# Attention with 128 steps of scores, exponentials and values: issuing probabilities times values for two key tiles together

## The chip, the cores and the metric

The kernel runs on 1 core of one Trainium2 chip. The metric is device microseconds (us) of one execution of the whole program; the time before is a median of three runs.

## The reference

x is 1024 tokens by 512 features. It is layer-normed to xn. An attention branch projects xn to 32 query heads and 8 key/value heads of 16 features each (four query heads share one key/value head), applies rotary embedding to queries and keys, and computes softmax(q k^T / 4) v over all 1024 keys, without a mask. A dense branch computes z = xn W^T + b, a low-rank product m with a clamped ratio of norms as its factor, and silu of the sum. The output is x + attention * silu(dense).

```python
scores = jnp.einsum('bqhd,bkhd->bhqk', q, k) / jnp.sqrt(jnp.float32(D))
probs = jax.nn.softmax(scores.astype(jnp.float32), axis=-1)
out = jnp.einsum('bhqk,bkhd->bqhd', probs, v).reshape(B, S, E)
...
x = x + s * g
```

## The kernel before

**Groups, steps and heads.** After a part that normalises, projects, rotates and splits queries and keys into bf16 parts (to about 104 us), the attention goes through KV = 8 groups g (one key/value head and its four query heads). A group has 16 steps s: half = s // 8 is the half of the queries (512 of them), kt = s % 8 the tile of 128 keys. In a step TensorE makes, for each of the four heads h, the scores of 128 keys by 512 queries (`score_cols(h)`, L868, matmul L875) into one of the three banks of `st`, which are used in turn. ScalarE takes the exponential of each (L526) into `probs`, which holds PB = 4 steps. `values(g, s)` (L827, matmuls L839) then multiplies the probabilities of step s with the values of its key tile: four heads side by side in four 32-column strips of the array, 128 rows deep, float32, accumulated over the 8 key tiles of a half in the bank `oT`. A float32 matmul shows as two passes, so one call of `values` is 8 matmul records.

**Row maxima.** The exponential needs a row maximum. While group g is computed, TensorE also makes the scores of group g+1 the other way round, 128 queries by 1024 keys (`score_rows`, L771, two matmuls at L777; two such blocks a step, called by `next_rows`), into the two halves of `sm`, in turn. VectorE reduces each (L595). GpSimd splits the maxima in two bf16 parts (L361, L364), TensorE turns them at steps 2 and 10 (`turn_maxima`, L794), ScalarE copies them (L508, L515) and SyncE's queue copies them into the query operand (L249, L276).

**What sets the order.** All order is written out by hand, one list of instructions for each engine, with semaphores. Within step s TensorE issues: score_cols(0), score_cols(1), score_rows, score_cols(2), `values` of step s-1, score_rows, score_cols(3). Three waits matter here. A score_cols may start when the exponential three banks back is done (`st_free`, L874). A score_rows may start when the row maximum two blocks back is done (`sm_free`, L775). `values` waits for the last exponential of its step (L830), and at the first key tile of a half also for `heads_out`. The exponentials of step s wait until the values of step s-4 have been taken (`pv_done`, L521).

**Heads out.** After the eighth key tile of a half ScalarE copies `oT` to `heads` (`evacuate`, L495, activation L500): at step 0 after head 2 for the second half of the group before, at step 8 after head 2 for the first half. TensorE turns the heads at steps 2 and 10 (`turn_heads`, L843, transposes L848), VectorE divides by the sums (L637, L640), GpSimd multiplies with the gate and adds (L390, L393). `group_values` on GpSimd (L367) writes the next group's values once the last `values` of a group is done.

**The last group** has no row maxima to prepare. In their place TensorE computes the dense branch of the last four token tiles in `late_unit` (L851, L857, L860), spread over the steps by `LATE_UNITS` (L114): two or three units of float32 in some steps, none in others. The last `values` stands behind the loop (L927).

Of the kernel before, what the change touches and what calls it, by code (L numbers as in the profile page):

```python
# [34 lines left out]
NT = S // P  # L35
# [41 lines left out]
MAX1_SLOT, MAX0_SLOT = 2, 10  # L77
# [3 lines left out]
def st_score(g, s, h):  # L81
    return ST_PER * g + 4 * s + h + (s >= MAX1_SLOT) + (s >= MAX0_SLOT)
# [36 lines left out]
def build(nc, x, wq, wk, wv, biases, bv, wT, b, A, B, p_sc, cosT, sinT, ident, identb, ones, out):  # L119
    ctx = ExitStack()  # L120
    with ctx:
# [71 lines left out]
        def pj(n):  # L193
            return oT[:, :] if n % 4 == 3 else st[:, n % 4, :]
# [28 lines left out]
        def dense(t):  # L223

            return z_sb[:, t, :] if t < TH else late_gate[:, t - TH, :]
# [206 lines left out]
        @block.scalar  # L432
        def _(act):
            act.dma_start(id_sb[:, :], ident).then_inc(id_in, 16)
            act.dma_start(wk_sb, wk.rearrange("(c p) n -> p c n", p=P)).then_inc(wk_in, 16)
            act.dma_start(wq_sb[:, :, 0:P], wq.rearrange("(c p) n -> p c n", p=P)[:, :, 0:P]).then_inc(wq0_in, 16)
            act.dma_start(bias[:, :, :], biases).then_inc(small_in, 16)
            act.dma_start(cos_sb, cosT).then_inc(tab_in, 16)
            act.dma_start(sin_sb, sinT).then_inc(tab_in, 16)

            for t in range(NT):
                act.wait_ge(pj_full, PJ_AT["xT", t] + 1)
                act.activation(xT[:, t // TH, :, t % TH * P:(t % TH + 1) * P],
                               pj(PJ_AT["xT", t]).rearrange("p (c n) -> p c n", c=NE), ACT.Copy).then_inc(pj_act, 1)

            def cast(n):

                act.wait_ge(rotated, n + 1)
                if n >= 3:
                    act.wait_ge(stacked[n - 3], 16 * len(Q_SLOTS))  # L450
                act.activation(parts[:, n % 3, 0, :], rot[:, n % 2, :], ACT.Copy).then_inc(part1, 1)  # L451
                act.wait_ge(left1, n + 1)
                act.activation(parts[:, n % 3, 1, :], rot[:, n % 2, :], ACT.Copy).then_inc(part2, 1)  # L453

            for n in range(len(halves) - 2):
                cast(n)
                if n in (5, 6):
                    hh = n - 5
                    e = PJ_AT["u", hh]
                    act.wait_ge(ffn_in, 80)  # L460
                    act.wait_ge(pj_full, e + 1)
                    act.activation(uT[:, hh * HALF:(hh + 1) * HALF], pj(e), ACT.Copy,
                                   scale=p_sb[:, 0:1]).then_inc(pj_act, 1)

            def gate_tanh_of(t):
                act.wait_ge(gate_in, t + 1)
                act.activation(m_sb[:, t % 3, :], dense(t), ACT.Tanh, scale=0.5).then_inc(gate_tanh, 1)

            def squares(t):

                n = PJ_AT["m", t]
                act.wait_ge(pj_full, n + 1)
                if t >= 3:
                    act.wait_ge(gate_done, t - 2)
                if t >= 1:
                    act.wait_ge(norm_done, 2 * t)
                act.activation(junk[:, 1, :], pj(n), ACT.Square,
                               accum_out=norms[:, t, 1:2]).then_inc(norm_done, 1)
                act.activation(m_sb[:, t % 3, :], pj(n), ACT.Copy).then_inc(pj_act, 1)
                act.wait_ge(pj_dve, emptied(PJ_AT["z", t])[1])  # L480
                act.activation(junk[:, 0, :], z_sb[:, t, :], ACT.Square,
                               accum_out=norms[:, t, 0:1]).then_inc(norm_done, 1)

            squares(0)
            gate_tanh_of(0)
            cast(len(halves) - 2)
            squares(1)
            act.wait_ge(pj_full, PJ_AT["max0", 0] + 1)
            act.activation(maxT[:, 0, :], pj(PJ_AT["max0", 0]).bitcast(BF16)[0:32, 0:P], ACT.Copy).then_inc(pj_act, 1)
            gate_tanh_of(1)  # L490
            cast(len(halves) - 1)
            squares(2)
            squares(3)

            def evacuate(g, half, n, free):  # L495

                act.wait_ge(pv_done, 16 * g + 8 * (half + 1))
                if free is not None:
                    act.wait_ge(sm_full, free)
                act.activation(heads[:, half, :], oT[:, :], ACT.Copy).then_inc(heads_out, 1)  # L500

            def step(g, first=False, last=False):
                for s in range(16):
                    if s == MAX1_SLOT:
                        act.wait_ge(st_full, st_max1(g) + 1)
                        if not first:
                            act.wait_ge(max_in, 16 * 2 * g)
                        act.activation(maxT[:, 1, :], st[:, st_max1(0) % 3, :].bitcast(BF16)[0:32, 0:P],  # L508
                                       ACT.Copy).then_inc(st_free, 1)
                    if s == MAX0_SLOT and last:  # L510
                        pass
                    elif s == MAX0_SLOT:
                        act.wait_ge(st_full, st_max0(g) + 1)
                        act.wait_ge(max_in, 16 * (2 * g + 1))
                        act.activation(maxT[:, 0, :], st[:, st_max0(0) % 3, :].bitcast(BF16)[0:32, 0:P],  # L515
                                       ACT.Copy).then_inc(st_free, 1)
                    for h in range(REP):
                        late = 1 if last and s >= MAX0_SLOT else 0
                        act.wait_ge(st_full, st_score(g, s, h) + 1 - late)
                        if h == 0 and not (first and s < PB):  # L520
                            act.wait_ge(pv_done, 16 * g + s - PB + 1)  # L521
                        if first and h == 0 and s in (1, 2):
                            act.wait_ge(part3, len(halves))
                        if first and h == 0 and s == 3:
                            act.wait_ge(stacked[len(halves) - 1], 16 * len(Q_SLOTS))
                        act.activation(probs[:, s % PB, h, :], st[:, (st_score(0, s, h) - late) % 3, :], ACT.Exp,  # L526
                                       scale=float(D) ** -0.5).then_inc(st_free, 1)
                        if first and (s, h) in ((1, 3), (3, 3)):
                            gate_tanh_of({1: 2, 3: 3}[s])
                        if last and (s, h) in ((3, 3), (7, 3), (10, 3), (15, 3)):  # L530
                            gate_tanh_of({3: 4, 7: 5, 10: 6, 15: 7}[s])
                        if s == 0 and h == 2 and not first:
                            evacuate(g - 1, 1, 2 * g - 1, sm_base(g - 1) + 2 * OUT1_SLOT + 1)
                        if s == 8 and h == 2:
                            evacuate(g, 0, 2 * g, None if first else sm_out0(g - 1) + 1)

            step(0, first=True)
            with act.Fori(1, LAST) as g:
                step(g)
            step(LAST, last=True)  # L540
            evacuate(LAST, 1, 2 * LAST + 1, SM_LAST["out1"] + 1)

# [164 lines left out]
        def _(pe):  # L707
# [119 lines left out]
            def values(g, s, exps, free):  # L827

                kt = s % NT
                pe.wait_ge(st_free, exps)  # L830
                if kt == 0:
                    if free is None and s == 0:
                        claim_bank(3)
                    if free is not None:
                        pe.wait_ge(heads_out, free)
                    if s == 0:
                        pe.wait_ge(v_ready, g + 1)
                for h in range(REP):
                    mm = pe.matmul(oT[h * VC:(h + 1) * VC, :], vg[:, kt, :], probs[:, s % PB, h, :],  # L839
                                   start=(kt == 0), stop=(kt == NT - 1))  # L840
                mm.then_inc(pv_done, 1)
# [21 lines left out]
            def step(g, first=False, last=False):  # L863
                for s in range(16):
# [41 lines left out]
                    if last and units:  # L906
                        late_unit(*units.pop(0))
                    score_cols(2)
                    if s > 0:
                        values(g, s - 1, st_score(g, s - 1, 3) + 1 - (1 if last and s - 1 >= MAX0_SLOT else 0),  # L910
                               None if first and s == 1 else 2 * g + (s - 1) // NT)
                    elif not first:
                        values(g - 1, 15, st_score(g - 1, 15, 3) + 1, None)
                    if last and units:
                        late_unit(*units.pop(0))
                    next_rows(2 * s + 1)
# [66 lines left out]
```

## Time and profile before

| | |
|---|---|
| Median of 3 runs | 495.08 us (494.57 to 496.36) |
| Span of the profiled execution, first to last instruction | 494.9 us |
| Instructions | 8174 |
| TensorE matmul busy | 477.9 us, 97% |
| VectorE busy | 373.0 us, 75% |
| ScalarE busy | 308.8 us, 62% |
| GpSimd busy | 92.2 us, 19% |

The page gives no time of its own for the profiled execution apart from its span. The span lies 0.2 us under the median of the runs, so sums can be made against either. L839 stands for line 839 of the kernel. PE is the matmul part of TensorE and PEld its weight loads, DVE is VectorE, ACT ScalarE, POOL GpSimd, SP SyncE. A row of the timeline gives the start, the length and the number of instructions it stands for; an idle time before it, and what ended that, follow in brackets. The recorded length of a pipelined matmul is longer than the time until the next can start, so distances between starts are what counts.

### The profile page before, as it was taken

The page shows a single profiled execution, that of the slowest core. Times are in us where ns is not written, and L with a number is a line of the kernel's source. Part 1 is how long each engine was busy: PE and PEld are TensorE (multiplying, and loading weights), DVE is VectorE, ACT ScalarE, POOL GpSimd, SP SyncE. Part 2 cuts the span into 40 slices and gives each one's busy share as a digit, 9 for nine tenths or more (in the row PEclk, how much of TensorE's full clock was granted, in tenths as well). Part 3 has the DMA queues.
Part 4 walks back from the last instruction along what each step waited for, and adds up shares of the span by engine and source line. Part 5 has one row for each costly group of instructions (what it writes and reads, how often), then busy time and mean ns, then how long its engine had stood idle before and what let it go on. Part 6 is the DMA issues. An engine that isn't in the chain of part 4 may idle for free.

```text
span 494.9 us, 8174 instructions
## 1 busy us (share of the span) xinstructions
PE 477.9 (97%) x2437; PEld 166.2 (34%) x2437; DVE 373.0 (75%) x401; ACT 308.8 (62%) x603; POOL 92.2 (19%) x160
## 2 busy tenths in 40 slices
PE   7995999999999999999999999999999999999994
PEld 3772444432333332333232323232333323333231
DVE  5643898989888888888888888888888888833433
ACT  2221112377767777767777776767676777766774
POOL 4573225550000010001000100010001001001553
PEclk9997999999999999999999999999999999999999
DMA  8899965550000000000000000000000000002010
GB/s 302 263 119 117 116 79 64 64 66 1 2 0 3 2 1 1 1 0 1 0 1 0 1 0 1 0 1 0 1 0 1 0 1 1 0 2 75 19 49 29
DMA packets 16980, 17.06 MB, mean 34 GB/s; under 512 B 3394, under 2 KB 14914, under 8 KB 16962
## 3 DMA queue, kind: packets, MB, share of 16 engines
q1 hardware_dynamic: 15332, 15.21, 18.3%
q10 hardware_dynamic: 1632, 1.64, 1.0%
q8 instruction: 9, 0.15, 0.1%
q14 instruction: 7, 0.06, 0.1%
HBM read 6.76 MB, written 2.10 MB: 18 GB/s over the span
## 4 chain that ended last, share of the span: by engine, by line
PE 83%; DVE 4%; DMA 4%; POOL 3%; ACT 2%; issue 2%; SPq 1%; DVEq 0%
PE oT L839 26%; PE sm L777 24%; PE st L875 23%; PE sm L857 3%; DMA kA<-arena 2%; PE oT L720 2%; PE st L720 2%; DMA x_sb<-in_x 1%; PE sm L848 1%; POOL arena L315 1%; ACT arena L526 1%; DVE arena L577 1%; DVE arena L575 1%; DVE arena L573 1%; PE sm L860 1%
## 5 line engine op out<-in xcount | busy, mean ns | idle before, releaser
L595 DVE TENSOR_REDUCE negmax<-sm 128x1 f32<-128x1024 f32 x256 | 303.8, 1220 | 63.0 <-PE sm L777 62.4
L526 ACT ACTIVATE arena<-st 128x512 f32<-128x512 f32 x512 | 268.1, 601 | 99.0 <-PE st L875 98.2
L777 PE MATMUL sm<-kA,qA 96*128 (+1 forms) x512 | 155.1, 384 | 7.0 <-DMA kA<-arena 5.3
L875 PE MATMUL st<-qA,kA 98*128 (+1 forms) x512 | 158.4, 380 | 1.6 <-ACT arena L526 1.4
L839 PE MATMUL oT<-arena,vg 128*32 128x512 f32 x1024 | 136.4, 605 | 0.7 <-ACT arena L526 0.7
L777 PEld LDWEIGHTS sm<-kA,qA 96*128 (+1 forms) x512 | 39.5, 97 | 149.0 <-issue 117.8
L875 PEld LDWEIGHTS st<-qA,kA 98*128 (+1 forms) x512 | 49.1, 97 | 92.2 <-ACT arena L526 41.4
L361 POOL TENSOR_TENSOR maxp<-negmax,consts 128x16 bf16<-128x16 f32 x16 | 3.4, 215 | 261.9 <-PE st L875 210.6
L839 PEld LDWEIGHTS oT<-arena,vg 128*32 128x32 f32 x1024 | 20.1, 108 | 37.2 <-issue 24.8
L451 ACT ACTIVATE arena<-arena 128x512 bf16<-128x512 f32 x10 | 6.3, 630 | 40.8 <-POOL arena L315 40.8
L674 DVE TENSOR_TENSOR xT_sb<-sm,b_sb 128x512 f32<-128x512 f32 x4 | 2.8, 692 | 21.1 <-PE sm L860 21.1
L315 POOL TENSOR_TENSOR arena<-arena 128x512 f32<-128x512 f32 x10 | 12.7, 1265 | 31.9 <-DVE arena L577 31.9
L720 PE MATMUL oT<-xT_sb,arena 128*128 128x512 f32 x32 | 17.3, 655 | 0.0
L857 PE MATMUL sm<-wT_sb,xT_sb 128*128 128x512 f32 x32 | 17.1, 615 | 0.0
L720 PE MATMUL st<-wT_sb,xT_sb 128*128 128x512 f32 x32 | 16.2, 591 | 0.0
L720 PE MATMUL st<-xT_sb,arena 128*128 128x512 f32 x32 | 15.6, 595 | 0.0
L453 ACT ACTIVATE arena<-arena 128x512 bf16<-128x512 f32 x10 | 6.3, 630 | 13.3 <-POOL arena L319 13.3
L390 POOL TENSOR_TENSOR gated<-scaled,z_sb 128x256 f32<-128x256 f32 x8 | 5.8, 730 | 41.1 <-DVE scaled L640 41.1
L324 POOL TENSOR_TENSOR arena<-arena 128x512 bf16<-128x512 f32 x10 | 11.9, 1185 | 5.9 <-ACT arena L453 5.9
L319 POOL TENSOR_TENSOR arena<-arena 128x512 f32<-128x512 f32 x10 | 11.5, 1155 | 6.1 <-ACT arena L451 6.1
L344 POOL TENSOR_TENSOR gam<-norms,consts 128x2 f32<-128x2 f32 x8 | 6.5, 812 | 30.4 <-DVE uT L681 28.3
L500 ACT ACTIVATE wkv<-oT 128x512 f32<-128x512 f32 x16 | 9.6, 598 | 3.6 <-PE oT L839 3.5
(88 smaller groups left out, 255.0 us busy)
## 6 DMA issues: line engine op xcount, KB each, us to landing
qA<-arena SPq DMA_DIRECT2D x48, 128.0 KB, 5.4
x_sb<-in_x SPq DMA_DIRECT2D x8, 256.0 KB, 6.5
kA<-arena SPq DMA_DIRECT2D x12, 128.0 KB, 6.6
wT_sb<-in_wT SPq DMA_DIRECT2D x1, 1024.0 KB, 8.0
out<-x_sb SPq DMA_DIRECT2D x1, 896.0 KB, 4.0
out<-x_sb SPq DMA_DIRECT2D x4, 224.0 KB, 2.0
arena<-in_wq SPq DMA_DIRECT2D x1, 768.0 KB, 11.1
arena<-in_cosT ACTq DMA_DIRECT2D x1, 512.0 KB, 7.4
```

The costliest lines, as they stand in the source:

```text
L315: pool.tensor_tensor(rot[:, n % 2, :], rot[:, n % 2, :], swp[:, n % 2, :], ALU.add).then_inc(rotated, 1)
L319: pool.tensor_tensor(rot[:, n % 2, :], rot[:, n % 2, :], parts[:, n % 3, 0, :], ALU.subtract).then_inc(left1, 1)
L324: pool.tensor_tensor(parts[:, n % 3, 2, :], rot[:, n % 2, :], parts[:, n % 3, 1, :], ALU.subtract).then_inc(part3, 1)
L344: pool.tensor_tensor(gam[:, t, :], norms[:, t, :], consts[:, 1:2].broadcast_to((P, 2)), ALU.pow).then_inc(pow_step, 1)
L500: act.activation(heads[:, half, :], oT[:, :], ACT.Copy).then_inc(heads_out, 1)
L526: act.activation(probs[:, s % PB, h, :], st[:, (st_score(0, s, h) - late) % 3, :], ACT.Exp, scale=float(D) ** -0.5).then_inc(st_free, 1)
L595: dve.tensor_reduce(negmax[:, half, r:r + 1], sm[:, bank, :], AX.X, ALU.max, negate=True).then_inc(sm_free, 1)
L720: mm = pe.matmul(pj(n), weight[:, c, columns], moving[:, c, :], start=(c == 0), stop=(c == NE - 1))
L777: mm = pe.matmul(sm[:, bank, kh * HALF:(kh + 1) * HALF], qA[0:KR, half, bass.ds(g, 1), h, qt * P:(qt + 1) * P] .rearrange("p a n -> p (a n)"),
L839: mm = pe.matmul(oT[h * VC:(h + 1) * VC, :], vg[:, kt, :], probs[:, s % PB, h, :], start=(kt == 0), stop=(kt == NT - 1))
L857: pe.matmul(sm[:, n % 2, 0:HALF], xT[:, 1, c, (t - TH) * P:(t - TH + 1) * P], wT_sb[:, c, :], start=(c == 0), stop=(c == NE - 1))
L875: pe.matmul(st[:, (st_score(0, s, h) - fewer) % 3, :], kA[:, bass.ds(g, 1), kt * P:(kt + 1) * P].rearrange("p a n -> p (a n)"), qA[:, half ...
```

## The change

TensorE no longer issues `values` once in each step. At each even step s it issues, in the same place behind score_cols(2), the values of steps s-2 and s-1 one right behind the other; at step 0 these are steps 14 and 15 of the group before. Odd steps have none, but for step 15 of the last group, which takes step 14; step 15's stand behind the loop as before. ScalarE copies the heads out a step later: after head 1 of step 1 and of step 9, in place of after head 2 of steps 0 and 8.

```diff
--- before.py
+++ after.py
@@ -529,9 +529,9 @@
-                        if s == 0 and h == 2 and not first:
+                        if s == 1 and h == 1 and not first:
                             evacuate(g - 1, 1, 2 * g - 1, sm_base(g - 1) + 2 * OUT1_SLOT + 1)
-                        if s == 8 and h == 2:
+                        if s == 9 and h == 1:
                             evacuate(g, 0, 2 * g, None if first else sm_out0(g - 1) + 1)
@@ -906,11 +906,13 @@
                     score_cols(2)
-                    if s > 0:
-                        values(g, s - 1, st_score(g, s - 1, 3) + 1 - (1 if last and s - 1 >= MAX0_SLOT else 0),
-                               None if first and s == 1 else 2 * g + (s - 1) // NT)
-                    elif not first:
-                        values(g - 1, 15, st_score(g - 1, 15, 3) + 1, None)
+                    if s == 0 and not first:
+                        for k in (14, 15):
+                            values(g - 1, k, st_score(g - 1, k, 3) + 1, None)
+                    elif s > 0:
+                        for k in ((s - 2, s - 1) if s % 2 == 0 else (14,) if last and s == 15 else ()):
+                            values(g, k, st_score(g, k, 3) + 1 - (1 if last and k >= MAX0_SLOT else 0),
+                                   None if first and k == 0 else 2 * g + k // NT)
```

## Rows read from the trace of the kernel before

**Rows 1.** The page: busy time by engine, and the granted clock by slice.
```profile
PE 477.9 (97%) x2437; PEld 166.2 (34%) x2437; DVE 373.0 (75%) x401; ACT 308.8 (62%) x603; POOL 92.2 (19%) x160
...
PEclk9997999999999999999999999999999999999999
```

**Rows 2.** The page: costliest groups (busy us, mean ns | idle before, releaser).
```profile
L595 DVE TENSOR_REDUCE negmax<-sm 128x1 f32<-128x1024 f32 x256 | 303.8, 1220 | 63.0 <-PE sm L777 62.4
L526 ACT ACTIVATE arena<-st 128x512 f32<-128x512 f32 x512 | 268.1, 601 | 99.0 <-PE st L875 98.2
...
L839 PE MATMUL oT<-arena,vg 128*32 128x512 f32 x1024 | 136.4, 605 | 0.7 <-ACT arena L526 0.7
```

**Rows 3.** Eight steps: length, busy us (count) of PE, PEld, DVE, ACT, POOL, then PEclk.
```profile
294.42:318.09 23.67, 23.62 (x135) 7.25 (x134) 19.59 (x19) 17.39 (x36) 0.88 (x3) 1.00 0.00 0
```

**Rows 4.** Timeline of an ordinary step, 259.3 to 262.6 us: start, length, instruction.
```profile
259.34 0.64 PE L839 MATMUL oT<-arena,vg 128*32 128x512 f32 x4
259.79 0.61 PE L839 MATMUL oT<-arena,vg 128*32 128x512 f32 x4
260.33 0.39 PE L777 MATMUL sm<-kA,qA 96*128 x1
260.56 0.38 PE L777 MATMUL sm<-kA,qA 96*128 x1
260.78 0.38 PE L875 MATMUL st<-qA,kA 98*128 x1
...
260.98 2.36 DVE L595 TENSOR_REDUCE negmax<-sm 128x1 f32<-128x1024 f32 x2 [0.48 <-PE sm L777]
261.19 2.06 ACT L526 ACTIVATE arena<-st 128x512 f32<-128x512 f32 x4 [0.77 <-PE st L875]
...
261.84 0.10 PEld L875 LDWEIGHTS st<-qA,kA 98*128 x1 [0.32 <-ACT arena L526]
261.86 0.38 PE L875 MATMUL st<-qA,kA 98*128 x1
262.17 0.62 PE L839 MATMUL oT<-arena,vg 128*32 128x512 f32 x2
```

**Rows 5.** Timeline, two float32 matmuls of the full array behind one another.
```profile
91.13 0.59 PE L720 MATMUL st<-xT_sb,arena 128*128 128x512 f32 x1
...
91.56 1.02 PE L720 MATMUL st<-xT_sb,arena 128*128 128x512 f32 x2
```

**Rows 6.** The chain that ended last, step 15 of the last group, 483.7 to 486.1 us.
```profile
483.71 0.99 PE oT L839 x8
...
485.07 0.61 ACT arena L526
485.67 0.05 issue
...
486.11 0.55 PE oT L839
```

**Rows 7.** Timeline of steps 0 to 7 of a group, 247.1 to 267.8 us.
```profile
247.08 1.07 PE L839 MATMUL oT<-arena,vg 128*32 128x512 f32 x8
248.30 0.60 ACT L500 ACTIVATE wkv<-oT 128x512 f32<-128x512 f32 x1 [0.21 <-PE oT L839]
...
251.82 0.39 PE L875 MATMUL st<-qA,kA 98*128 x1
252.49 0.38 PE L875 MATMUL st<-qA,kA 98*128 x1
...
253.67 1.06 PE L839 MATMUL oT<-arena,vg 128*32 128x512 f32 x8
...
267.84 1.07 PE L839 MATMUL oT<-arena,vg 128*32 128x512 f32 x8
```

**Rows 8.** The chain that ended last, two neighbouring late steps of the last group.
```profile
452.73 1.06 PE sm L857 x2
456.50 1.06 PE sm L857 x2
```

## The prediction, made before the changed kernel was run

> **What bounds the kernel now.** I read the page's busy times first. TensorE has 97%, VectorE 75%, ScalarE 62%, and the granted clock is at its upper level (2.4 GHz) in nearly every slice [rows 1]; no step of the change touches the clock. The costliest groups then say who waits for whom: ScalarE's exponentials sat idle 98 us for TensorE's scores, VectorE's row maxima 62 us, while TensorE's `values` waited 0.7 us in all [rows 2]. Half a group of eight steps takes 23.67 us, of which TensorE is busy 23.62 [rows 3]. So TensorE's order of work is the bound from 104 to 437 us, and an average says no more than that. What matters is how much slack stands behind it, and for this the timeline of one step is read [rows 4].
>
> Take the start of `values` as zero (259.34). The second pass starts at 0.45, score_rows at 0.99 and 1.22, score_cols(3) at 1.44; the next step's two score_cols and its score_rows follow, score_cols(2) at 2.52, and the next `values` at 2.83. That is an ordinary step, **2.83 us**; five of them take 14.17 us (253.67 to 267.84), so two take 5.67 [rows 7]. Two things are to be seen. First, `values` costs time at its edges: score_cols(2) to `values` takes 0.31, where a score otherwise takes 0.22 (260.56 to 260.78), and the second pass of `values` takes 0.54 until score_rows may start, where float32 passes of the full array follow one another after 0.43 [rows 5]. Second, the weight load of score_cols(2) at 261.84 waited for an exponential, and its matmul started only 0.02 later: TensorE lost nothing by it, but there was nothing to spare.
>
> **Part 1: the seam that disappears.** In a pair, the first `values` takes 0.45 + 0.43 = 0.88 until the second, if the second's weights load behind the running pass as those of a second pass do now, and the second takes 0.99. So score_rows starts at 1.87. A pair saves TensorE one leaving (0.54 - 0.43 = 0.11) and one entering (0.31 - 0.22 = 0.09), 0.20 us in all. `values` has no row in which it follows itself. Bounds: 0.45 + 0.41 = 0.86 at best (if the strips overlap by the 0.02 over which four heads start), 0.99 if each call keeps its edge. I take 0.88, since the pass to pass rows are the same kind of work.
>
> **Part 2: the three banks.** TensorE is now away from scores for 1.87 us, not 0.99. Before it leaves, three banks are full at most; ScalarE empties them in some 1.5 us and stands idle. When TensorE comes back, scores pile up again behind the exponentials. I follow the chain, with the pair's start as zero:
> - score_rows at 1.87, score_cols(3) 0.45 behind it (260.33 to 260.78) at 2.32 [rows 4].
> - Its exponential starts 0.41 after the matmul's start (260.78 to 261.19): 2.73.
> - The fourth exponential from there starts 2.06 - 0.60 = 1.46 later [rows 2, 4]: 4.19. It is that of score_cols(2) of the odd step, and ends at 4.79.
> - A waiting weight load follows the end of an exponential after 0.05 [rows 6]: 4.84. The score that waits there is score_cols(1) of the next even step, since with three banks it needs the bank of three scores back.
> - Behind it, on TensorE's one queue, stand the two matmuls of score_rows, score_cols(2) and the next pair: 3 x 0.22 + 0.31 = 0.97, so the next pair starts at **5.81**.
>
> TensorE's own work would have let it start at 5.67 - 0.20 = 5.47. The pair saves 0.20 and waits 0.34: **+0.14 us a pair**. That this chain can bind is seen at the end of the kernel before, where steps 14 and 15 of the last group have nothing but scores and `values`: there the chain goes from `values` to score, exponential, 0.05, score, `values`, in 2.40 us a step [rows 6], although ScalarE and TensorE each have less than that to do.
>
> VectorE's chain is close behind. With two halves of `sm`, the second score_rows of the odd step waits for the maximum of the block behind the pair: its second matmul starts at 2.10 and the maximum 0.42 later (260.56 to 260.98), at 2.52; it takes 1.22 [rows 2, 4], so the block then starts at 3.79, with the same 0.05, where TensorE would be ready at 3.62 (5.47 less seven matmuls at 0.22 and an entering). This wait of 0.17 lies within the time that score_cols(1) loses anyway, as the next pair could still start at 3.79 + 1.85 = 5.64. The next block needs the next maximum: 2.52 + 1.14 + 1.22 + 0.05 = 4.93 (1.14 is 2.36 less 1.22, start to start), and the pair 0.75 later, at 5.68. So VectorE is 0.13 behind the binding chain, and it is what would be late next.
>
> **Part 3: the copy of the heads.** It has the same 0.6 us on ScalarE. At present it sits in a gap: ScalarE had waited 0.21 us for `values` [rows 7]. After the change it stands between the third and the fourth exponential of the chain above, so it adds 0.48 (one more ScalarE start to start) to the chain. The bank that it holds up is now that of score_cols(0) of step 2 or 10, as the turned maxima take one of the ring's places. From the pair at step 0 (or 8): fourth exponential at 4.67, done and seen at 5.32; score_cols(0) to score_cols(1), with the turned heads between them, 0.67 [rows 7]; then 0.97 to the next pair: **6.96**. Before, the same two steps take 253.67 - 247.08 = 6.59 [rows 7]. So **+0.37 us** at each of these places. Bounds: 0.14 (the copy in a gap after all) and 0.14 + 0.48.
>
> **What moves at no cost.** `probs` holds four steps; the exponentials of an even step now need a pair taken two steps earlier, which is some 3 us before they ask. GpSimd's group_values starts 0.9 us later and is needed a step later than now; GpSimd is 19% busy [rows 1]. The turned maxima, their copies and their DMAs by SyncE's queue keep their places behind score_rows and `st`. If this cover fell, the wait would be at score_cols(0) of steps 0 and 8.
>
> **The sum.** From the pair at step 2 of group 0 to the one at step 0 of the last group there are 55 distances of two steps: 13 with a copy and turned heads, 42 ordinary. 42 x 0.14 = 5.9 and 13 x 0.37 = 4.8. In the first two steps of group 0 a `values` is gone and the row maxima take the place of the bound: -0.5 (between -1.2 and 0). In the last group late units of float32 make TensorE the bound in most steps, 3.77 us from one to the next [rows 8], so the seam is won there (0.20 each), while its steps without units pay more than 0.14, by up to 0.4; seven pairs, between -1.5 and +2.6, taken as 0. Sum +10.2 us, on a median of 495.1 (the span is 0.2 less): **505.3 us**.
>
> **The rivals.**
> *TensorE alone is the bound (faster).* The busy shares speak for it: at 97% against 62% and 75% [rows 1], whatever TensorE saves should be saved. The time: 63 pairs x -0.20 = -12.6, **482.5 us**. It decides if the chain of part 2 is shorter by 0.34 or more, which needs one of its terms to be wrong; each is a row. The Trainium skill, TensorEngine Tiling (Array Packing), Key Properties, says that changing the tiling mode drains the array; by that rule alone two changes of mode in four go away, and the sum would be this rival's. The trace agrees that the edges cost (0.09 and 0.11) [rows 4, 5].
> *The seam stays.* The second `values` waits as score_rows does now: 0.99, not 0.88. Then every pair starts 0.11 to 0.12 later, since the seam lies on the binding chain: 63 x 0.12 = 7.6 more, **513 us**. For it: no row shows `values` behind `values`. Against: its own two passes follow in 0.45.
> *A wash.* The chain is shorter by 0.14, for instance as VectorE's and ScalarE's waits leave TensorE's queue in another order than I wrote; then the saved edges pay for the waits: **495 to 497 us**.
> *The copy hides.* ScalarE has idle time left in every second step, and the boundary pairs pay no more than the ordinary ones: 55 x 0.14 - 0.5 = +7.2, **502 us**. Against it stands the place that the copy is given, among four exponentials in a row.
>
> **How the numbers follow.** A difference of 0.5%, 2.5 us, is about what a measurement of this kernel can tell from none. Chances: my forecast 0.66, seam stays 0.12, copy hides 0.06, wash 0.07, TensorE alone 0.09. Slower: 0.84. Same: 0.07. Faster: 0.09. The low end is the copy that hides with the lower bounds of group 0, of the last group and of the seam: 7.7 - 1.2 - 1.5 - 55 x 0.02 = +3.9, 499; the high end is the seam that stays, 513. That leaves out the wash and TensorE alone, 0.16.
>
> **What would show it.** Right: the distance from one pair to the next is 5.8 in ordinary steps and 6.9 to 7.0 where heads are turned; score_rows follows the pair's start by 1.87; ScalarE's idle time for scores stands in one piece of over 1 us each second step; and L875's weight loads wait longer for L526, at score_cols(1) of even steps. TensorE's busy share falls by some points although it has less to wait out at edges. L777's weight loads now wait for row maxima. Wrong: a distance of 5.5 (TensorE alone), or a start of the second `values` 1.0 behind the first (the seam stays), or no longer wait at step 2 than elsewhere (the copy hides).

## The result, and the profile after

The changed kernel takes **509.04 us** (median of 4 runs, 508.06 to 512.06), the kernel before in the same session 495.48 us (494.57 to 496.36). The ratio is 1.028, 95% interval 1.024 to 1.032: slower by 13.6 us, where 10.2 had been worked out. The two profiled executions differ by 13.3 us (spans of 494.9 and 508.2). The forecast named the sign and the mechanism. Its sum had nothing for the turns of the loop and for VectorE's extra work in group 0, and somewhat too little at the turned heads and at both ends.

The page of the changed kernel: the busy times, the two groups that wait for TensorE, and TensorE's own groups with the weight loads of L875 (columns as in [rows 1, 2]).

```profile
PE 477.5 (94%) x2437; PEld 172.6 (34%) x2437; DVE 368.6 (73%) x401; ACT 304.9 (60%) x603; POOL 92.5 (18%) x160
...
L595 DVE TENSOR_REDUCE negmax<-sm 128x1 f32<-128x1024 f32 x256 | 298.7, 1218 | 77.0 <-PE sm L777 73.2
L526 ACT ACTIVATE arena<-st 128x512 f32<-128x512 f32 x512 | 267.2, 604 | 118.5 <-PE st L875 117.1
L875 PE MATMUL st<-qA,kA 98*128 (+1 forms) x512 | 164.5, 381 | 9.3 <-ACT arena L526 8.1
...
L839 PE MATMUL oT<-arena,vg 128*32 128x512 f32 x1024 | 123.3, 598 | 0.7 <-ACT arena L526 0.7
L875 PEld LDWEIGHTS st<-qA,kA 98*128 (+1 forms) x512 | 49.2, 97 | 107.9 <-ACT arena L526 57.4
```

The page of the kernel before has for the scores (L875):

```profile
L875 PE MATMUL st<-qA,kA 98*128 (+1 forms) x512 | 158.4, 380 | 1.6 <-ACT arena L526 1.4
...
L875 PEld LDWEIGHTS st<-qA,kA 98*128 (+1 forms) x512 | 49.1, 97 | 92.2 <-ACT arena L526 41.4
```

Against [rows 1, 2]: the values' busy time fell from 136.4 to 123.3 us, which fits edges that went away, though a recorded length runs over the start of the next matmul, and the distances below are the measure. In return ScalarE's exponentials waited 19 us longer for scores, VectorE's maxima 11 us longer, and the scores on TensorE now wait for exponentials themselves: 8.1 us of matmul idle time where it had been 1.4, and weight loads held back for 57.4 us (41.4 before). All three engines wait for one another a little longer, and no busy share says so. I read this as too few banks for the longer absence; no run changes the number of banks (three of `st`, two halves of `sm`), so more banks as the cure are not shown.

One pair of steps in the middle of group 3 shows where the waits are (timeline: start, length, instruction, in brackets the idle time before it).

```profile
240.95 1.92 PE L839 MATMUL oT<-arena,vg 128*32 128x512 f32 x16
...
242.81 0.60 PE L777 MATMUL sm<-kA,qA 96*128 x2
...
243.45 4.62 DVE L595 TENSOR_REDUCE negmax<-sm 128x1 f32<-128x1024 f32 x4 [1.19 <-PE sm L777]
243.67 3.58 ACT L526 ACTIVATE arena<-st 128x512 f32<-128x512 f32 x7 [1.73 <-PE st L875]
...
244.34 0.38 PE L875 MATMUL st<-qA,kA 98*128 x1
244.81 0.11 PEld L777 LDWEIGHTS sm<-kA,qA 96*128 x2 [0.40 <-issue]
...
245.78 0.10 PEld L875 LDWEIGHTS st<-qA,kA 98*128 x1 [0.40 <-ACT arena L526]
...
246.76 0.64 PE L839 MATMUL oT<-arena,vg 128*32 128x512 f32 x4
```

The reader is to see four things. The pair is away for 242.81 - 240.95 = 1.86 us (1.87 had been worked out). ScalarE stands idle for 1.73 us in one piece, VectorE for 1.19, where they had 0.77 and 0.48 a step [rows 4]. Then the weight load of score_rows at 244.81 comes 0.47 after the score ahead of it, where a matmul otherwise follows after 0.22. The row says "issue"; that it waited for the maximum of the block behind the pair is my reading, and half_max bears it out: with shorter maxima this score_rows follows after 0.22 (247.00 to 247.22). Last, the weight load at 245.78 waits for the fourth exponential, that of score_cols(2): this is score_cols(1) of the even step, the place that the prediction named, at 4.83 after the pair's start (4.84 had been worked out). The next pair starts at 246.76, **5.81** after the first, where two steps had taken 5.67.

The pairs around a turn of the loop and the two steps behind it, steps 14, 0, 2, 4 and 6 (timeline, TensorE alone):

```profile
246.76 1.92 PE L839 MATMUL oT<-arena,vg 128*32 128x512 f32 x16
252.80 1.92 PE L839 MATMUL oT<-arena,vg 128*32 128x512 f32 x16
259.83 1.92 PE L839 MATMUL oT<-arena,vg 128*32 128x512 f32 x16
265.64 1.92 PE L839 MATMUL oT<-arena,vg 128*32 128x512 f32 x16
271.45 1.06 PE L839 MATMUL oT<-arena,vg 128*32 128x512 f32 x8
```

The distances are 6.04, 7.03, 5.81 and 5.81. The ordinary ones stand as worked out; 7.03 had been put at 6.96; **6.04 had been put at 5.81** and is a surprise that the first group of experiments does not explain and no_loop does. The six turns of the loop lie between 6.01 and 6.10.

From the first pair's start (111.52) to the one at step 0 of the last group (449.65) it is 338.1 us; the same two places of the kernel before lie 325.0 us apart. That is 13.1 us over 55 distances, where the sum had 10.7.

### The profile page after: what moved, and what is told of

Same layout as the page of the kernel before. It is cut to its first block, busy times and chain, and to the rows that moved or that the text cites. A ratio compares the mean times of both kernels' runs of the same rounds, so it can differ in the third digit from the quotient of the medians.

```text
span 508.2 us, 8180 instructions
## 1 busy us (share of the span) xinstructions
PE 477.5 (94%) x2437; PEld 172.6 (34%) x2437; DVE 368.6 (73%) x401; ACT 304.9 (60%) x603; POOL 92.5 (18%) x160
## 4 chain that ended last, share of the span: by engine, by line
PE 73%; ACT 7%; issue 5%; DVE 5%; DMA 4%; POOL 3%; SPq 2%; ACTq 0%; DVEq 0%
PE oT L839 23%; PE sm L777 21%; PE st L875 20%; ACT arena L526 4%; PE sm L857 3%; DMA kA<-arena 2%; PE oT L720 2%; ACT wkv L500 2%; PE st L720 2%; DVE negmax L595 2%; DMA x_sb<-in_x 1%; PE sm L848 1%; SPq L262 1%; POOL arena L315 1%; DVE arena L577 1%
## 5 line engine op out<-in xcount | busy, mean ns | idle before, releaser
L595 DVE TENSOR_REDUCE negmax<-sm 128x1 f32<-128x1024 f32 x256 | 298.7, 1218 | 77.0 <-PE sm L777 73.2
L875 PE MATMUL st<-qA,kA 98*128 (+1 forms) x512 | 164.5, 381 | 9.3 <-ACT arena L526 8.1
L777 PE MATMUL sm<-kA,qA 96*128 (+1 forms) x512 | 154.9, 384 | 13.1 <-DMA kA<-arena 6.2
L839 PE MATMUL oT<-arena,vg 128*32 128x512 f32 x1024 | 123.3, 598 | 0.7 <-ACT arena L526 0.7
L875 PEld LDWEIGHTS st<-qA,kA 98*128 (+1 forms) x512 | 49.2, 97 | 107.9 <-ACT arena L526 57.4
L839 PEld LDWEIGHTS oT<-arena,vg 128*32 128x32 f32 x1024 | 26.6, 109 | 62.9 <-issue 39.0
L453 ACT ACTIVATE arena<-arena 128x512 bf16<-128x512 f32 x10 | 6.3, 630 | 13.3 <-POOL arena L319 13.3
L602 DVE SCALAR_TENSOR_TENSOR xT_sb<-m_sb,gam,xT_sb 128x512 f32<-128x512 f32 x4 | 4.7, 1178 | 8.6 <-POOL gam L353 8.6
```

What stands on the lines that cost most here:

```text
L595: dve.tensor_reduce(negmax[:, half, r:r + 1], sm[:, bank, :], AX.X, ALU.max, negate=True).then_inc(sm_free, 1)
L777: mm = pe.matmul(sm[:, bank, kh * HALF:(kh + 1) * HALF], qA[0:KR, half, bass.ds(g, 1), h, qt * P:(qt + 1) * P] .rearrange("p a n -> p (a n)"),
L875: pe.matmul(st[:, (st_score(0, s, h) - fewer) % 3, :], kA[:, bass.ds(g, 1), kt * P:(kt + 1) * P].rearrange("p a n -> p (a n)"), qA[:, half ...
```

## The experiments

**What holds the scores back.** Four kernels take work off ScalarE, VectorE or both. The diffs are against the changed kernel; before_both has both edits against the kernel before. In half_exp, half_both and before_both half of the probabilities is left out; in half_max, half_both and before_both the maxima are taken over half of the keys.

```diff
# half_exp
-act.activation(probs[:, s % PB, h, :], st[:, (st_score(0, s, h) - late) % 3, :], ACT.Exp,
+act.activation(probs[:, s % PB, h, 0:256], st[:, (st_score(0, s, h) - late) % 3, 0:256], ACT.Exp,
# half_max
-dve.tensor_reduce(negmax[:, half, r:r + 1], sm[:, bank, :], AX.X, ALU.max,
+dve.tensor_reduce(negmax[:, half, r:r + 1], sm[:, bank, 0:HALF], AX.X, ALU.max,
# half_both, before_both: the two together
```

Expected of half_exp:

> The changed kernel with exponentials of the first 256 columns of each block only (the other half of the probabilities is left out). A start-to-start of ScalarE falls from 0.48 to about 0.27. Theory (ScalarE's chain through three banks ends last, VectorE's is a few hundredths behind): VectorE's chain takes over at once, pairs go from 5.81 to 5.75 to 5.78, total 505 to 508. Rival, ScalarE alone is in the way: pairs fall to TensorE's own 5.47, total near 490. Rival, nothing but the pair's length on TensorE counts: no change at all.

Expected of half_max:

> The changed kernel with row maxima over the first 512 of 1024 keys only. Theory: ScalarE's chain binds in ordinary pairs, which stay at 5.81; where VectorE had extra work (group 0's gates, steps 0 to 6) some 1 us is won in all: 507 to 509. Rival, VectorE's chain is the binding one: pairs fall by 0.1 or more, total 500 or less.

Expected of half_both:

> The changed kernel with both halvings. Theory: both chains are out of the way and TensorE's own work is the bound: pairs at 5.47, 0.34 less than 5.81, total near 509 - 55 x 0.34 - 1 = 489 or lower. Rival, a third thing (a wait on the values, the queue, the seam) binds: pairs stay above 5.7.

Expected of before_both:

> The kernel before with both halvings (exponentials of 256 columns, row maxima over 512 keys), as the control. Theory: before the change TensorE's own work is the bound in the groups, so steps stay at 2.83 us and the total within 3 us of 495 (the ends and group 0 may win a little). Against the changed kernel with both halvings it is slower by what the seam saves, about 55 x 0.20 = 11 us. Rival, the halving by itself speeds TensorE up: the steps get shorter.

Measured:

| | total us | ratio to before | an ordinary pair, us |
|---|---|---|---|
| changed kernel | 509.04 | 1.028 (1.024 to 1.032) | 5.81 |
| half_max | 506.68 | 1.022 (1.018 to 1.026) | 5.81 |
| half_exp | 501.39 | 1.011 (1.007 to 1.016) | 5.75 |
| half_both | 475.05 | 0.958 (0.954 to 0.962) | 5.43 |
| before_both | 488.88 | 0.985 (0.982 to 0.988) | 5.67 (two steps) |

Two neighbouring pairs of half_exp, in group 3 (timeline):

```profile
236.71 1.92 PE L839 MATMUL oT<-arena,vg 128*32 128x512 f32 x16
242.46 1.92 PE L839 MATMUL oT<-arena,vg 128*32 128x512 f32 x16
```

The same of half_both:

```profile
248.44 1.92 PE L839 MATMUL oT<-arena,vg 128*32 128x512 f32 x16
...
253.87 1.92 PE L839 MATMUL oT<-arena,vg 128*32 128x512 f32 x16
```

In the groups of TensorE's loop, either relief alone gives an ordinary pair 0.06 us or nothing; both together give 0.38. So two chains end within 0.06 us of each other there, ScalarE's through three banks of `st` at 5.81 and VectorE's through two halves of `sm` at 5.75, and TensorE's own work lies far below both. Group 0 is written out in front of the loop, and there VectorE's chain ends at 5.67. Two pairs of half_exp in group 0:

```profile
134.20 1.92 PE L839 MATMUL oT<-arena,vg 128*32 128x512 f32 x16
...
139.87 1.92 PE L839 MATMUL oT<-arena,vg 128*32 128x512 f32 x16
```

The experiment on the turn of the loop, below, shows where these 0.08 us stand.

The totals of the relieved kernels came out lower than expected. half_exp was expected at 505 to 508 us and took 501.39: between the two places named above (the first pair and the one at step 0 of the last group) it gained 4.5 us, and another 2.5 in the last group, which I had left out. half_max was expected at 507 to 509 and took 506.68, with 1.1 us gained between the two places. half_both was expected near 489 or lower and took 475.05. There the two steps with turned heads fell from 7.03 and 6.95 to 6.20 and 6.13, far more than the 0.34 that I had taken for every pair, and the last group gained 2.5 us as well.

The rival that made ScalarE alone the cause falls with half_exp, the one that made VectorE alone the cause falls with half_max, and the one that made the pair's own length count falls with half_both.

before_both is the control, and its ordinary steps stay at 2.83 us: before the change TensorE's own order was the bound there, and halving alone does not speed them up. Its total was expected within 3 us of 495 and came out 7 lower. Of this, 3.7 us lie between the two places named above: at the steps with turned heads (3.54 us, not 3.76, between two values) and at the steps into 0 and 8 (2.83, not 2.91). There the exponentials did count; the rest lies in the ends. Between before_both and half_both stands what the pairs are worth with these two waits out of the way: 5.67 - 5.43 = **0.24 us a pair**, 13.8 us in all (12.2 of them between the two places). The prediction had 0.20. The Trainium skill, TensorEngine Tiling (Array Packing), Key Properties, has a change of tiling mode drain the array. The 0.24 us agree in so far as two changes of mode fewer take less time; what the array does meanwhile no run shows. The section PSUM Bottleneck of the same page of the Trainium skill warns that tiling speeds up TensorE and leaves the emptying of its banks as it was. All kernels here tile alike, so that warning is not tested; what the runs show is that less work in emptying the banks takes the changed kernel from 509 to 475 us.

**Which chain, by order alone.** Nothing is left out here; score_cols(3) and score_rows change places behind each pair.

```diff
+                    if s % 2 == 0: score_cols(3)
                     next_rows(2 * s + 1)
-                    score_cols(3)
+                    if s % 2 == 1: score_cols(3)
```

> The changed kernel with score_cols(3) ahead of the score_rows block right behind each pair, nothing left out. It takes 0.45 us out of ScalarE's chain and puts 0.22 into VectorE's. Theory of two chains: ScalarE's would end at 5.36, VectorE's, which measured waits put at 5.77, ends at 5.99: pairs of about 6.0 us, slower than the changed kernel by about 55 x 0.18 = 10 us, 519. Rival, ScalarE's chain alone: pairs at 5.47 to 5.6, total 491 to 498.

Measured: 516.70 us, ratio 1.042 (1.040 to 1.044), pairs 5.97 apart. The timeline of TensorE in score_first:

```profile
241.77 1.92 PE L839 MATMUL oT<-arena,vg 128*32 128x512 f32 x16
243.63 0.39 PE L875 MATMUL st<-qA,kA 98*128 x1
243.86 0.60 PE L777 MATMUL sm<-kA,qA 96*128 x2
...
245.85 0.60 PE L777 MATMUL sm<-kA,qA 96*128 x2 [0.32 <-DVE negmax L595]
246.29 0.81 PE L875 MATMUL st<-qA,kA 98*128 x3
```

ScalarE is served 0.45 us earlier, VectorE 0.23 later, and the kernel gets slower by 7.7 us, where 10 had been expected (a pair loses 0.16, not 0.18, and those with turned heads 0.06 to 0.14). At 245.85 the wait carries VectorE's name, and stands as idle time of the matmuls themselves. What is won for one chain is lost by the other.

**The copy of the heads.**

```diff
-                        if s == 1 and h == 1 and not first:
+                        if s == 0 and h == 2 and not first:
...
-                        if s == 9 and h == 1:
+                        if s == 8 and h == 2:
```

> The changed kernel with the copy of the heads back at its old places, after head 2 of steps 0 and 8. My theory: ScalarE stands idle there anyway while TensorE does the pair, the copy starts about 0.2 us behind the pair's end and is over before the next score can be used, so the two steps with turned heads fall from 6.95 to 7.04 us to about 6.75, 13 times 0.2 to 0.3: 3 to 4 us less than the changed kernel, 505 to 506 us. Ordinary pairs stay 5.81. Rival (the copy was hidden already, the long distance there is the turned heads' and maxima's own work): no change, 509.

Measured: 506.79 us, ratio 1.022 (1.018 to 1.025), 2.2 us less than the changed kernel. In its timeline the copy, and the pairs around it:

```profile
155.01 1.92 PE L839 MATMUL oT<-arena,vg 128*32 128x512 f32 x16
...
157.09 0.60 ACT L500 ACTIVATE wkv<-oT 128x512 f32<-128x512 f32 x1 [1.35 <-PE oT L839]
...
161.89 1.92 PE L839 MATMUL oT<-arena,vg 128*32 128x512 f32 x16
```

The copy starts in ScalarE's idle stretch and the distance is 6.88 in both places, not 7.03 and 6.95; I had expected 6.75. In half_exp, with the copy at its later place and short exponentials, it is 6.88 too; in half_max, with short maxima, it stays at 7.03 and 6.95; in half_both it is 6.13 to 6.20. So ScalarE's chain with the copy ends at 6.95 or later and VectorE's at 6.88, and VectorE's takes over when the copy moves back. The later place of the copy was the worse one, but it is worth only some 2 us of the 13.6: 2.2 by the medians, 1.5 between the two places of the traces.

**The turn of the loop.**

```diff
-            with pe.Fori(1, LAST) as g:
-                step(g)
+            for g in range(1, LAST):
+                step(g)
```

> The changed kernel with TensorE's loop over groups 1 to 6 written out in full, the same instructions in the same order on it, and nothing changed on the other engines. The distance from the pair of step 14 to the pair of step 0 of the next group is 6.01 to 6.11 us in the changed kernel, 0.2 to 0.3 above the ordinary 5.81. Theory: TensorE's sequencer turns the loop (register work and a branch of 0.2 us) behind step 15, which has no values any more under which it could run ahead. Written out, the distance is 5.81 and some 1.2 to 1.5 us are won in all: 507.5. Rival, it is a wait on row maxima or exponentials that would stand there anyway: the distance stays at 6.0.

Measured: 505.51 us, ratio 1.019 (1.016 to 1.021), 3.5 us less than the changed kernel. The pairs of steps 14 and 0 in its timeline:

```profile
243.48 1.92 PE L839 MATMUL oT<-arena,vg 128*32 128x512 f32 x16
249.29 1.92 PE L839 MATMUL oT<-arena,vg 128*32 128x512 f32 x16
```

That is 5.81, not 6.04. The changed kernel's own timeline has the wait between these two pairs (TensorE and its weight loads):

```profile
250.85 0.10 PEld L875 LDWEIGHTS st<-qA,kA 98*128 x1
251.06 1.03 PE L875 MATMUL st<-qA,kA 98*128 x3
251.48 0.32 PEld L875 LDWEIGHTS st<-qA,kA 98*128 x2 [0.53 <-issue]
252.03 0.24 PEld L777 LDWEIGHTS sm<-kA,qA 96*128 x2 [0.23 <-issue]
```

"issue" means that the profile shows nothing that the engine waited for. By itself the word does not decide, since it also stands at 244.81, where I read a wait for a maximum; no_loop decides, as with the loop gone this wait is gone. By the order of the code, the kernel before turned its loop while a `values` of one microsecond was running; step 15 of the changed kernel has none.

Written out, two more distances shrink by 0.08 us: from step 6 to 8 it is 5.81, not 5.89, and from step 0 to 2 it is 6.95, not 7.03. Between the same two places as above the trace has 335.7 us, 2.4 less than with the loop, and these distances account for it: 1.4 to 1.5 at the six turns, as expected, and 12 times 0.08. The medians say 3.5. The rest lies outside: in the profiled executions the first pair starts at 109.05 in no_loop and at 111.52 in the changed kernel, after code that both share.

no_loop also shows where the 0.08 us stand. The score_rows of the odd step, with VectorE and the weight loads (compare 243.45 and 244.81 of the changed kernel above):

```profile
245.98 4.62 DVE L595 TENSOR_REDUCE negmax<-sm 128x1 f32<-128x1024 f32 x4 [1.19 <-PE sm L777]
...
247.26 0.11 PEld L777 LDWEIGHTS sm<-kA,qA 96*128 96x128 bf16 x2 [0.32 <-DVE negmax L595]
```

The maximum of 1.22 us ends at 247.20 and the load starts some 0.05 us later. With the loop it started 0.13 later. That holds in all 48 such places of groups 1 to 6, and group 0, which was never in the loop, has 0.05 in both kernels. So the extra 0.08 is a cost of the looped code on TensorE, and not of VectorE. Why it costs that, no run shows; register work for the group's number is my guess.

**A seam where nobody has to wait.** If it is the time away from scores that costs, a seam that is saved with hardly more time away must be a gain. The turned maxima are a 32-column matmul too. turn_by_values puts the values of steps 0 and 8 right ahead of them, last_only pairs the values only in steps 2, 4, 6 and 8 of the last group, where the dense units stand in place of the row maxima; both against the kernel before.

```diff
# last_only
-                    if s > 0:
+                    if last and s < 9 and s > 0:
+                        for k in (s - 2, s - 1) if s % 2 == 0 else ():
+                            values(g, k, st_score(g, k, 3) + 1, 2 * g + k // NT)
+                    elif s > 0:
                         values(g, s - 1, ...
# turn_by_values
-                    if s > 0:
+                    if s in (1, 9) and not (last and s == 9):
+                        pass
+                    elif s > 0:
                         values(g, s - 1, ...
...
                     score_cols(3)
                     if last and units:
                         late_unit(*units.pop(0))
+                    if s in (1, 9) and not (last and s == 9):
+                        values(g, s - 1, st_score(g, s - 1, 3) + 1, None if first and s == 1 else 2 * g + (s - 1) // NT)
# turn_and_last: both, but the last group's values of step 0 go with its pairs; turn_last_no_loop: the same, and TensorE's loop written out
```

Expected of last_only:

> The kernel before with pairs only in steps 2, 4, 6 and 8 of the last group, where late units make TensorE the bound and the changed kernel's trace gained 0.33 us a pair on the kernel before. Theory: 4 pairs x 0.33 = 1.3 us less than before, 494.0 against 495.4, ratio 0.997. Rival, the gain there is given back in steps 9 to 15, as it was in the changed kernel: no difference.

Expected of turn_by_values:

> The kernel before with the values of steps 0 and 8 issued at the end of steps 1 and 9, right ahead of the turned maxima (also a 32-column matmul), in 15 places; all other values stay one per step. Theory: what the pairs won by a seam is won here, 0.1 to 0.2 us a place, and TensorE is away from scores for hardly more than one values, so no chain ends later: 1.5 to 3 us less than before, ratio 0.994 to 0.997. Rival, any bunching next to steps with turned heads is paid back in waits for exponentials, as ScalarE had to catch up there: no change or slower by up to 3 us.

Expected of turn_and_last:

> The run before this one and the pairs of the last group (last_only) together. Theory: the two sum, 2.8 to 4.3 us less than before, ratio 0.991 to 0.994. Rival: only last_only's 1.3 us remain, ratio 0.997, or less.

Expected of turn_last_no_loop:

> turn_and_last with TensorE's loop over groups 1 to 6 written out. Theory: two steps of each group (7 and 15) still take 2.91 us there, 0.08 above the ordinary 2.83, while TensorE's sequencer does register work; written out they take 2.83, about 12 x 0.08 = 1 us less than turn_and_last's 491.3, ratio 0.988 to 0.990 against before. Rival, the longer program costs as much in fetching instructions: no difference from turn_and_last.

| | total us | ratio to before, 95% interval |
|---|---|---|
| last_only | 494.78 | 0.9974 (0.9962 to 0.9985) |
| turn_by_values | 493.24 | 0.9945 (0.9927 to 0.9962) |
| turn_and_last | 491.33 | 0.9906 (0.9889 to 0.9923) |
| turn_last_no_loop | 490.16 | 0.9876 (0.9857 to 0.9896) |

The values of steps 15, 0 and 1 in turn_by_values, and the turned maxima between them (timeline):

```profile
295.88 1.06 PE L839 MATMUL oT<-arena,vg 128*32 128x512 f32 x8
...
296.76 0.22 PE L794 MATMUL st<-idb_sb,maxp 128*32 128x128 bf16 x1
...
298.54 1.05 PE L839 MATMUL oT<-arena,vg 128*32 128x512 f32 x5
```

The maxima follow the start of the values by 0.88, as one `values` follows another inside a pair; from step 15's values (292.12) to step 1's (298.54) it is 6.42 us, where it had been 6.59 [rows 7]. 13 times 0.17 is 2.2 us, and the trace has 322.8 us where it had 325.0. All four kernels are faster than the kernel before with intervals clear of 1, though each by less than 2%, and within the intervals the parts sum. The last one **beats both kernels**, by 6.0 us against the kernel before of its own session and by 18.9 us against the 509.04 of the changed kernel's. Its gain over turn_and_last, 1.2 us, compares two sessions. Between the same two places their traces differ by 1.9 us, twice what had been expected: the steps into 0 and 8 are at 2.83 and not 2.91, and the steps with turned heads are shorter by 0.08 too (3.68, not 3.76, from the values of step 15 to those of step 0).

## Why the prediction was right, point by point

**The bound and the seam.** That TensorE's order of work bounds the ordinary steps is shown by before_both (2.83 us a step with both other engines relieved); at the turned heads the exponentials already counted for 0.22 us. The second `values` follows the first by 0.88 as worked out. The pair's own saving is 0.24, not 0.20: the second call's two passes follow at 0.43, not 0.45, and the 0.23 between the two matmuls right behind `values`, otherwise 0.22, stands once and not twice. In the groups no number of the sum hung on this, as the chain bound.

**The three banks.** Right to 0.01 us: the weight load that waits, its place in the order, and 5.81 for the pair. It is the part of the sum that carried it, 42 x 0.14 = 5.9.

**VectorE's chain.** It was put at 5.68. In group 0 of half_exp, where TensorE's code is written out, it is 5.67; in the loop's groups it is 5.75. The missed piece is the 0.08 us that the looped code adds between the end of a row maximum and the weight load that waits for it (0.13 in place of the 0.05 that I had taken). That is why half_exp gained 0.06 and not 0.13 a pair there. At the turned heads it is the same: this chain takes 6.80 in group 0 of half_exp and of heads_back, and 6.88 in the loop's groups. The prediction had not worked VectorE's chain out for these steps, and heads_back showed it.

**The copy.** Right that it pays in the chain, +0.37 worked out against +0.44 and +0.36 measured (7.03 and 6.95 against 6.59); the 0.08 more from step 0 to 2 is the loop's, as no_loop has 6.95 in both places. half_max, where ScalarE's chain is left alone, keeps both distances, so the 6.96 that was worked out for that chain holds. But VectorE's chain ends at 6.88, so what the copy costs beyond it is only 0.07 to 0.15 each, and most of the 0.37 would be paid without the copy too.

**What was mis-sized.** 13.1 against 10.7 over the 55 distances. Ordinary ones give 5.9, as worked out. The remaining 2.4 us are: 1.0 at the loop's turns, which the sum did not have; 0.5 at the steps with heads, which it had too small; and 0.9 in the first two distances, in group 0. There VectorE still adds the gates of the dense branch in between row maxima. The first pairs of the changed kernel start here:

```profile
111.52 1.92 PE L839 MATMUL oT<-arena,vg 128*32 128x512 f32 x16
...
117.78 1.92 PE L839 MATMUL oT<-arena,vg 128*32 128x512 f32 x16
```

This is 6.26, and the next is as long, 0.46 above 5.81 each. VectorE in that stretch of the changed kernel:

```profile
114.02 1.23 DVE L595 TENSOR_REDUCE negmax<-sm 128x1 f32<-128x1024 f32 x1 [0.97 <-PE sm L777]
115.16 0.68 DVE L608 SCALAR_TENSOR_TENSOR z_sb<-m_sb,z_sb 128x512 f32<-128x512 f32 x1
115.76 3.48 DVE L595 TENSOR_REDUCE negmax<-sm 128x1 f32<-128x1024 f32 x3
```

The gate (L608) adds 0.60 us to VectorE's chain, which in group 0 ends at 5.67: together 6.27, as measured. VectorE's chain is 0.14 us behind the binding one there, so 0.46 of the 0.60 show. In half_max both distances are 5.81, as VectorE's chain is out of the way. The prediction had called VectorE's chain "what would be late next" and then did not ask where VectorE had more to do than in an ordinary step; that step of it failed, and so did the one that took the code of the loop to cost nothing. The first two steps of group 0, put at -0.5, gave -0.3 (the first pair at 111.52, the same place before at 111.81). The same code starts its first pair at 109.05 in no_loop and at 112.24 in heads_back, so that term is not tested.

**The last group** had been taken as 0, between -1.5 and +2.6, and gave +0.5: 51.8 us from its first pair to the last values, against 51.3. Under the dense units a pair won 0.33 us, more than the 0.20 taken; why the seam is worth more there was not tried by itself. The steps from 8 on gave it back, and 0.5 more: the last stretch alone, from the pair at step 14 to the last values, grew by 0.86 us, where up to 0.4 had been allowed a place. last_only keeps the first part alone: 49.8 us for the same stretch, 1.6 less than before.

**The rivals.** "The seam stays" falls by the 0.88. "TensorE alone" is what half_both shows, once both waits are out of the way. "A wash" and "the copy hides" fall by the distances.

## What to carry to other kernels

A seam between two kinds of matmul is worth closing only as far as it does not keep TensorE away from the engines that it feeds: lay out the chain from its return to its next departure, one waiting instruction at a time, with the number of banks as the number of blocks that one may run ahead, and do so for every engine that it feeds. A busy share of 97% says that TensorE is the bound now; it does not say that work taken off it is won. Where two kinds of work can be put side by side without a longer absence (here one `values` beside one small transpose), the same seam is a gain.

## What the runs showed of the hardware that I had not expected

- Relief of one engine that feeds from TensorE gave 0.06 us a pair or nothing, of both 0.38: half_exp and half_max together would have promised 10 us, and half_both gave 34.
- A turn of the loop on TensorE costs 0.20 to 0.29 us in the changed kernel, where no long matmul stands ahead of it (6.01 to 6.10 against 5.81). With short exponentials and maxima (half_both) it costs 0.12. Written out, the longer program cost nothing that shows.
- In the looped groups of the kernel before, the steps into 0 and into 8 take 2.91 and not 2.83, though the loop turns only at 0. In each of these 12 places a weight load of score_cols starts 0.13 us after the exponential that it waits for; in turn_last_no_loop it is 0.05 and the steps take 2.83. In before_both the steps take 2.83 with the loop in place, so this 0.08 shows only where that wait is the late one.
- A waiting weight load starts 0.05 us after the instruction that it waits for, be it ScalarE's exponential [rows 6] or VectorE's maximum (no_loop, and group 0 of every kernel), and in the looped code at some places 0.13 after. Which waits of the loop pay the 0.08 no run sorts out: in the changed kernel all 48 for a maximum do, and of those for an exponential a minority.
